# One packet for the categories, row groups loaded first, and the weight loads shared out differently

## What is computed

```python
def _L0_cond_ref(x, cat_ids, W, b):
    selected_W = W[cat_ids]
    selected_b = b[cat_ids]
    return jnp.einsum('bsd,bdh->bsh', x, selected_W) + selected_b[:, None, :]

x = x + _L0_cond_ref(x, itok_B_0_63, L0_cond_W, L0_cond_b)
```

## Time and profile before

| | |
|---|---|
| median of 3 runs | 105.71 us (105.23 to 106.25) |
| the profiled execution, device time | 105.33 us |
| its span in the profile | 103.6 us |
| TensorE busy | 87.4 us |
| DMA | 31.26 MB, 302 GB/s over the span |
| granted TensorE clock | full in every slice |

### The profile page before, as it was taken

How to read it: one execution, slowest core, us unless ns; L and a number is a source line. 1 busy time by engine, 2 the same in 40 slices (tenths; PEclk the granted TensorE clock), 3 DMA queues, 4 the chain that set the end, 5 groups by cost and what they waited for, 6 DMA issues and landing times.

```text
span 103.6 us, 3047 instructions
## 1 busy us (share of the span) xinstructions
PE 87.4 (84%) x786; PEld 58.2 (56%) x786; DVE 57.0 (55%) x137; ACT 55.0 (53%) x97; POOL 62.0 (60%) x103
## 2 busy tenths in 40 slices
PE   0039958867889977979999999999999999999990
PEld 0017725534555745637576767666667676666650
DVE  1085514233998879075646463737292828282841
ACT  0001927326436609279577665766666757585600
POOL 5000019889989898999999998984053597000000
PEclk9999999999999999999999999999999999999999
DMA  0587994999999999999999999999997799993353
GB/s 10 143 273 220 291 314 167 334 324 331 354 332 350 353 347 345 348 356 399 351 391 372 394 367 400 373 388 350 373 392 271 227 333 320 331 322 114 108 202 105
DMA packets 13825, 31.26 MB, mean 302 GB/s; under 512 B 1840, under 2 KB 7664, under 8 KB 13808
## 3 DMA queue, kind: packets, MB, share of 16 engines
q0 software_dynamic: 7456, 25.17, 69.0%
q1 hardware_dynamic: 4832, 4.59, 13.5%
q10 hardware_dynamic: 1520, 1.31, 4.4%
HBM read 25.30 MB, written 8.39 MB: 325 GB/s over the span
## 4 chain that ended last, share of the span: by engine, by line
PE 54%; DMA 16%; issue 15%; POOL 6%; POOLq 3%; DVE 2%; ACT 1%; ACTq 0%; SPq 0%; DVEq 0%
PE mm_ps L527 36%; DMA w_all<-in_L_cond_W 12%; PE xt_ps L444 10%; PE mm_ps L513 6%; POOL w_all L162 5%; DMA cat_col_i<-in_itok_B 4%; POOLq L162 2%; PE xt_ps L527 2%; POOL rows L171 1%; POOLq L156 1%; ACT w_slot L292 1%; DVE rows L413 0%; DVE same_ahead L361 0%; DVE has_place L373 0%; PE mm_ps L458 0%
## 5 line engine op out<-in xcount | busy, mean ns | idle before, releaser
L527 PE MATMUL mm_ps<-w_slot,xT 128*64 128x256 f32 x496 | 57.8, 380 | 5.3 <-ACT w_slot L292 4.0
L292 ACT COPY w_slot<-w_all 128x512 f32 x64 | 38.7, 620 | 32.8 <-SPq L207 20.7
L527 PEld LDWEIGHTS mm_ps<-w_slot,xT 128*64 128x64 f32 x496 | 34.5, 137 | 22.9 <-issue 4.9
L162 POOL DMA_DIRECT2D w_all<-in_L_cond_W x56 | 33.4, 599 | 9.8 <-SPq L207 5.6
L413 DVE TENSOR_TENSOR rows<-mm_ps,rows 128x512 f32<-128x512 f32 (+1 forms) x32 | 21.6, 674 | 23.9 <-PE mm_ps L527 23.0
L292 DVE COPY w_slot<-w_all 128x512 f32 x64 | 26.6, 447 | 12.1 <-SPq L207 12.1
L444 PE MATMUL xt_ps<-ident,rows 128*128 128x128 f32 x128 | 19.0, 298 | 0.4 <-DMA rows<-in_x 0.4
L171 POOL DMA_DIRECT2D rows<-in_x x14 | 11.0, 786 | 13.5 <-SPq L207 12.9
L444 PEld LDWEIGHTS xt_ps<-ident,rows 128*128 128x128 f32 x128 | 15.3, 151 | 6.5 <-issue 5.3
L304 ACT COPY xT<-xt_ps 128x512 f32<-128x512 f32 x32 | 17.1, 584 | 0.0
L175 POOL DMA_DIRECT2D out<-rows x22 | 16.1, 736 | 1.1 <-issue 1.1
(11 more groups left out here) (39 smaller groups left out, 13.3 us busy)
## 6 DMA issues: line engine op xcount, KB each, us to landing
w_all<-in_L_cond_W POOLq DMA_DIRECT2D x56, 256.0 KB
rows<-in_x POOLq DMA_DIRECT2D x14, 512.0 KB, 8.1
out<-rows POOLq DMA_DIRECT2D x22, 256.0 KB, 7.0
out<-rows SPq DMA_DIRECT2D x8, 256.0 KB, 3.7
rows<-in_x SPq DMA_DIRECT2D x2, 512.0 KB, 4.5
w_all<-in_L_cond_W ACTq DMA_DIRECT2D x4, 256.0 KB, 4.8
w_all<-in_L_cond_W SPq DMA_DIRECT2D x4, 256.0 KB, 5.8
out<-rows SPq DMA_DIRECT2D x2, 128.0 KB, 1.7
```

Source lines behind the costliest of these rows:

```text
L162: engine.dma_start(w_all[:, n, :, :], weights[bass.ds(c, 1), :, :].rearrange("c (k p) h -> p (c k) h", p=P), **how).then_inc(first_w_loade ...
L292: copy(w_slot[:, PAIR * p + half, :, :].rearrange("p k h -> p (k h)"), w_all[:, bass.ds(c, 1), :, :].rearrange("p c k h -> p (c k h)")).th ...
L527: last = T.matmul(to[HALF * half:HALF * (half + 1), :], xT[:, slot, k, j, :], w_slot[:, j, k, :], start=False, stop=(k == K - 1), skip_gro ...
```

## The change

The categories come once, as one row of 128 numbers on one partition (`cats_i`, SyncE). VectorE casts them to bf16, and two small matmuls spread them in PSUM: `cat_row` (128x128, by a row of ones) and `cat_col_ps` (128x1). VectorE and the later plan steps read these from PSUM. The row of ones is made by VectorE and copied by ScalarE at the very start. `cat_col_i` and its transfer are gone.

SyncE issues the rows of groups 0, 1 and 2 with the bias, without a wait between them. Loads 0 and 2 are ScalarE's, 1 and 3 SyncE's; GpSimd has all loads from 4 on, and begins when one load is reported. GpSimd reads the next packed word one load ahead. It stores a whole group by one transfer of 524,288 bytes. Rows of groups 5 and 6 come after loads 25 and 31 (24 and 29 before), and the stores of groups 0 to 4 come later in the order of loads. From load 12 on a load waits for the one eight before it. Groups 11 to 15 are stored as before.

```diff
-FIRST_X = 2
-FIRST_LOADS = 8
-REPORTED_FIRST = 5
+FIRST_X = 3
+FIRST_LOADS = 4
+REPORTED_FIRST = 1
-X_AFTER_LOAD = {3: 13, 4: 19, 5: 24, 6: 29, 7: 33, ...}
-STORE_AFTER_LOAD = {0: 33, 1: 37, 2: 40, 3: 43, 4: 46, 5: 51, 6: 59}
+X_AFTER_LOAD = {3: 13, 4: 19, 5: 25, 6: 31, 7: 33, ...}
+STORE_AFTER_LOAD = {0: 37, 1: 40, 2: 43, 3: 46, 4: 48, 5: 51, 6: 59}
...
-            sp.dma_start(cat_row_i[:, :], cat.partition_broadcast(P)).then_inc(cats_loaded, 16)
+            sp.dma_start(cats_i[:, :], cat.rearrange("(a b) -> a b", a=1)).then_inc(cats_loaded, 16)
             load_rows(sp, 0)
             sp.dma_start(bias_nat[:, :], bias).then_inc(bias_loaded, 16)
-
-            sp.wait_ge(cats_loaded, 32)
             for g in range(1, FIRST_X):
                 load_rows(sp, g)
...
-            def store_group(g):
-                for q in range(QUADS_IN_GROUP * g, QUADS_IN_GROUP * (g + 1)):
-                    pool.wait_ge(sums_added, q + 1)
-                    store_quad(pool, q, stored[g % X_SLOTS])
+            def store_sums(g):
+                pool.wait_ge(sums_added, QUADS_IN_GROUP * (g + 1))
+                store_group(pool, g)
...
             pool.wait_ge(w_loads_done, REPORTED_FIRST)
-            load_rows(pool, FIRST_X)
             for n in range(FIRST_LOADS, C):
                 if n % WORD == 0 and n > FIRST_LOADS:
-                    word = words_read(...)
+                    word = next_word
+                if n % WORD == WORD - 1 and n + 1 < C:
+                    next_word = list_word(n // WORD + 1)
...
-            act.dma_start(cat_col_i[:, :], cat.rearrange("(b a) -> b a", a=1)).then_inc(cats_loaded, 16)
-
-            act.wait_ge(cats_loaded, 32)
-            load_weights(act, 0, words_read(mybir.EngineType.Activation, cat_row_i[0:1, 0:1], C - 1)[0])
+            act.wait_ge(ones_set, 1)
+            nc.scalar.copy(ones_row[:, :], ones_f[:, :]).then_inc(ones_ready, 1)
+
+            act.wait_ge(cats_loaded, 16)
+            load_weights(act, 0, words_read(mybir.EngineType.Activation, cats_i[0:1, 0:1], C - 1)[0])
...
-            dve.wait_ge(cats_loaded, 32)
-            step(V.tensor_copy(cat_col[:, :], cat_col_i[:, :]))
+            dve.wait_ge(cats_loaded, 16)
+            V.tensor_copy(cats[:, :], cats_i[:, :]).then_inc(plan_step, 1)
+            dve.wait_ge(plan_products, 1)
+            step(V.tensor_copy(cat_col[:, :], cat_col_ps))
...
+            pe.wait_ge(plan_step, PLAN_STEPS["cats"])
+            pe.wait_ge(ones_ready, 1)
+            T.matmul(cat_row, ones_row[:, :], cats[:, :], start=True, stop=True)
+            T.matmul(cat_col_ps, cats[:, :], ones[0:1, :], start=True, stop=True).then_inc(plan_products, 1)
```

More of the change, by code:

```diff
@@ L29 @@
 FAR = 1000.0
-PLAN_STEPS = {"samples": 6, "first": 9, "list": 12, "slots": 15, "bias": 16}
-X_AFTER_LOAD = {3: 13, 4: 19, 5: 24, 6: 29, 7: 33, 8: 37, 9: 40, 10: 43, 11: 46, 12: 48, 13: 51, 14: 55, 15: 60}
-STORE_AFTER_LOAD = {0: 33, 1: 37, 2: 40, 3: 43, 4: 46, 5: 51, 6: 59}
+PLAN_STEPS = {"samples": 6, "cats": 7, "first": 10, "list": 13, "slots": 16, "bias": 17}
+X_AFTER_LOAD = {3: 13, 4: 19, 5: 25, 6: 31, 7: 33, 8: 37, 9: 40, 10: 43, 11: 46, 12: 48, 13: 51, 14: 55, 15: 60}
+STORE_AFTER_LOAD = {0: 37, 1: 40, 2: 43, 3: 46, 4: 48, 5: 51, 6: 59}
 POOL_GROUPS = 11
@@ L67, in build_cond_residual @@
     out_pairs = out.rearrange("(t h) s d -> (h s) t d", h=PAIR)
+    out_groups = out.rearrange("(g p h) s d -> g (h s) p d", p=PAIRS_IN_GROUP, h=PAIR)
     with ExitStack() as ctx:
@@ L89, in build_cond_residual @@
         ones = sb("ones", [P, 1], BF16)
+        ones_f = sb("ones_f", [1, P])
         powers = sb("powers", [P, WORD])
-        cat_row_i = sb("cat_row_i", [P, B], I32)
-        cat_col_i = sb("cat_col_i", [P, 1], I32)
+        cats_i = sb("cats_i", [1, B], I32)
+        cats = sb("cats", [1, B], BF16)
+        ones_row = sb("ones_row", [1, P], BF16)
         cat_col = sb("cat_col", [P, 1])
@@ L124, in build_cond_residual @@
         loads_ps = mm_ps[1][0:1, 0, LIST_WORDS:LIST_WORDS + 1]
+        cat_row = mm_ps[3][:, 0, 0:B]
+        cat_col_ps = mm_ps[3][:, 0, B:B + 1]
         bias_ps = [mm_ps[r % BANKS][0:ROWS, 0, :] for r in (2, 4, 6, 8)]
@@ L131, in build_cond_residual @@
         consts_ready = sem("consts_ready")
+        ones_set = sem("ones_set")
+        ones_ready = sem("ones_ready")
         plan_step = sem("plan_step")
@@ L166, in stores_until @@
         def stores_until(g):
-            return 16 * QUADS_IN_GROUP * (g // X_SLOTS + 1)
+            return 16 * (g // X_SLOTS + 1)
         def load_rows(engine, g):
@@ L176, in store_quad, with store_group @@
                              rows[:, g % X_SLOTS, PAIR * n:PAIR * (n + 1), :]).then_inc(done, 16)
+        def store_group(engine, g):
+            engine.dma_start(out_groups[g], rows[:, g % X_SLOTS, :, :]).then_inc(stored[g % X_SLOTS], 16)
         def store_pair(engine, p, done):
@@ L240, in _, with list_word @@
                       allow_small_or_imprecise_dtypes=True).then_inc(consts_ready, 1)
[L241 to L245 removed]
+            def store_sums(g):
+                pool.wait_ge(sums_added, QUADS_IN_GROUP * (g + 1))
+                store_group(pool, g)
+            def list_word(w):
+                return words_read(mybir.EngineType.Pool, load_words[0:1, w:w + 1], 2 ** (WORD * BITS) - 1)[0]
             pool.wait_ge(plan_read, 1)
[L249 to L250 removed]
+            word = list_word(FIRST_LOADS // WORD)
             pool.wait_ge(w_loads_done, REPORTED_FIRST)
[L253 removed]
             for n in range(FIRST_LOADS, C):
                 if n % WORD == 0 and n > FIRST_LOADS:
[L256 to L257 removed]
+                    word = next_word
+                if n % WORD == WORD - 1 and n + 1 < C:
+                    next_word = list_word(n // WORD + 1)
                 if n == CERTAIN_LOADS:
@@ L275, in _ @@
                     if after == n:
-                        store_group(g)
+                        store_sums(g)
             for g in range(len(STORE_AFTER_LOAD), POOL_GROUPS):
-                store_group(g)
+                store_sums(g)
         def slots_of(engine, g, half):
@@ L347, in _ @@
             V = nc.vector
+            V.memset(ones_f[:, :], 1.0).then_inc(ones_set, 1)
             V.memset(ones[:, :], 1.0).then_inc(plan_step, 1)
@@ L356, in _ @@
             assert steps[0] == PLAN_STEPS["samples"]
-            dve.wait_ge(cats_loaded, 32)
-            step(V.tensor_copy(cat_col[:, :], cat_col_i[:, :]))
+            dve.wait_ge(cats_loaded, 16)
+            V.tensor_copy(cats[:, :], cats_i[:, :]).then_inc(plan_step, 1)
+            steps[0] += 1
+            assert steps[0] == PLAN_STEPS["cats"]
+            dve.wait_ge(plan_products, 1)
+            step(V.tensor_copy(cat_col[:, :], cat_col_ps))
             dve.wait_ge(consts_ready, 2)
-            step(V.scalar_tensor_tensor(out=same_ahead[:, :], in0=cat_row_i[:, :], scalar=cat_col[:, 0:1],
+            step(V.scalar_tensor_tensor(out=same_ahead[:, :], in0=cat_row, scalar=cat_col[:, 0:1],
                                         in1=is_ahead[:, :], op0=ALU.is_equal, op1=ALU.mult,
@@ L375, in _ @@
             step(V.tensor_scalar(place[:, :], place_ps, FAR, first_here[:, 0:1], ALU.add, ALU.mult))
-            dve.wait_ge(plan_products, 2)
+            dve.wait_ge(plan_products, 3)
             V.tensor_copy(load_words[:, :], mm_ps[1][0:1, 0, 0:LIST_WORDS + 1]).then_inc(plan_read, 1)
-            V.tensor_scalar(same[:, :], cat_row_i[:, :], cat_col[:, 0:1], None, ALU.is_equal).then_inc(plan_step, 1)
+            V.tensor_scalar(same[:, :], cat_row, cat_col[:, 0:1], None, ALU.is_equal).then_inc(plan_step, 1)
             V.tensor_scalar(place_powers[:, :], powers[:, :], place[:, 0:1], None, ALU.mult).then_inc(plan_step, 1)
```

10 lines of the change are left out of this document (5 added, 5 removed).

## The result

The changed kernel took 102.33 us (median of 4 runs, 101.54 to 103.11) against 105.66 us; its ratio to the kernel before is 0.9656, 95% interval 0.9575 to 0.9736. The profiled execution took 101.54 us, the shortest of the four, and 99.9 of them are its span.

The account below looks back on a forecast made before the run. Load 31's landing, set by the bytes ahead of it, plus 0.91 us and a 58.09 us tail bounds the span. Landing 4.7 us earlier gives 98.9 us, with 1.73 outside it 100.6 us; range 99.0 to 103.2.

Parts of the forecast that it names:

- part 4: Load 31's landing: at 39.9 us against 44.60, a gain of 4.7 us, with bounds of 3.6 and 5.8.
- early transfers stay poor: Rival, 17 in 100: early DMA stays slow and most of the early gain is lost; time about 103 us.
- The bound: Whole kernel: the span is load 31's landing, plus 0.91 us to its matmul, plus 58.09 us of tail.
- Part 1, the order of bytes: Weight queue: group 6 rows behind load 31 and no category broadcast leave 11.60 MB ahead of load 31, 0.59 MB gained.
- Part 2, the early filling: First 19 us: data from 3.2 us at 300 GB/s, 342 from 12 us on; 5.03 MB moved against 3.99.
- part 3: GpSimd's start: plan ready at 5.7 us, GpSimd starts at about 8.6, its first data come at 10.5; the hole is closed.
- the cover I had reckoned: Early queue: SyncE's and ScalarE's 2.69 MB last until 12.2 us, covering GpSimd's first data at 10.5 by 1.7 us.
- the price of the packet: Category steps of the plan: they cost nothing under the cover; without it each microsecond would cost one.
- Part 5, TensorE's own row: Groups 0 to 4: without waits TensorE is ready at 38.9 us, loads allow 40.8, so loads decide by 1.9.
- Part 6, nothing late next: After load 31: load 37 has 2.7 us of slack, group 10 rows come at 57.9 us, wanted at 62; store and word zero.
- The signs: Right: no hole at 15-17 us, GpSimd's load at 8-9, over 4.7 MB by 19 us. Wrong: under 300 GB/s after 12.
- Slower by the low clock: Rival, 5 in 100: TensorE stays at its lower level, 4.0 us more for each such group; three give about 108 us.

Follow-up runs that it names:

- experiment 1: The changed kernel with the kernel before's tables: rows of groups 5 and 6 behind loads 24 and 29, stores where they were; 103.86 us, ratio 0.9844.
- experiment 2: The kernel before with only the change's two tables for the order of rows and stores; 104.28 us against 105.42, ratio 0.9906.
- experiment 8: The changed kernel with rows of group 2 issued by GpSimd behind load 7, and no wait of GpSimd for a reported load before load 4; 100.18 us.
- experiment 5: The changed kernel with rows of group 2 issued by GpSimd behind load 7, not by SyncE ahead of the weights; 101.46 us, ratio 0.9669.
- Experiments 8 and 11: The changed kernel with rows of group 2 behind load 7 and no gate for GpSimd, measured on two chips; 100.18 us, then 99.83 us.
- Experiment 7: The changed kernel with the old category transfers (broadcast and column) and ScalarE's table load behind its loads again; 104.90 us against 105.34, ratio 0.9966.
- experiment 9: The kernel before with only the change's categories (one packet, spread by TensorE) and rows of group 1 not waiting for them; 104.24 us against 105.87.
- experiment 6: The changed kernel with two stores for a group, as before, and no word read ahead; 101.95 us, ratio 0.9692.
- experiment 3: The changed kernel without GpSimd's wait for a reported load before load 4; median 101.78 us over seven runs, in two heaps.

## Why the prediction was right, and where it was off

The forecast was 100.6 us, 5.1 below the median of before; measured are 102.33, 3.3 below it. The mechanism held, and the size was too large: 102.33 lies outside the 99.5 to 101.7 that the bounds of part 4 gave, and inside the range only by the room left for the rival "early transfers stay poor". Part of this is spread: the profiled execution (101.54) is the shortest of the four, 0.8 below their median, and it misses the forecast by 0.9. The repeat on another chip gave 101.60, a gain of 4.3. The sum is checked against the profiled execution below.

**The bound** (load 31, 0.91 us, a tail of 58.09 us) held to the last tenth: 0.91 and 58.1 us in the changed kernel, and 58.9 to 59.0 for the two together in every experiment whose load 31 the chain shows.

**Part 1, the order of bytes:** 1.5 us by the sum; experiment 1 shows 1.5 us by the medians and 1.7 to 2.7 by the gains, experiment 2 shows 1.1. Right.

**Part 2, the early filling,** is the term that was mis-sized. I took 300 GB/s from 3.2 to 12 us and 342 after that, 5.03 MB by 19 us; 4.81 MB were moved. The first half was even better than assumed (311 GB/s from 4 to 11 us), but from 12 to 19 us, where I had taken 342, there were 285, and 292 in the repeat. The 0.22 MB are 0.65 us. The rate after that was 338 to 339 and not 342 (0.2 us), and together with the remainder of the table load 31 landed at 40.89 and not at 39.9.

The sentence behind the 342 is in part 3: GpSimd "issues 262 KB in 0.71 us (2.82 / 4), 372 GB/s, faster than 342". That is the pace inside one burst. It leaves out GpSimd's pauses between bursts; with them ten loads took 8.64 us, 303 GB/s, in the change and in its repeat. From about 12 us on, when the bytes queued by SyncE and ScalarE were used up, the DMA engines then had no more than that to move. In experiment 8 GpSimd's pace was 346 GB/s, and 342 were moved from 12 to 19 us. In experiment 5 the pace was the same 346, but only 316 were moved. No experiment changed the pace alone, so this cause is argued and not shown.

**Part 3, GpSimd in time:** the plan came earlier than thought (4.94 us, not 5.7), since the packet landed 1.4 us after its issue, below the lower end of my bounds, 1.7. But the gate did not open with SyncE's last issue. I had priced load 0 at nothing; it took 5.80 us (5.37 to 5.80 in four executions), because it shares the DMA engines with three row groups (4.84 us with two, experiment 5). So GpSimd started at 9.90 and not at 8.6 us. That is inside the cover I had reckoned (10.3 us), but the queue emptied sooner than I thought: 2.69 MB were queued, and at the rates of the windows they were moved by about 11.3 us, not 12.2, since the early rate was above 300. GpSimd's first data, 1.9 us behind 9.90, came at 11.8. Experiments 8 and 11, where GpSimd starts at 6.6 us, moved 0.4 to 0.5 MB more by 19 us.

**Part 3, the price of the packet.** "The new steps of the plan cost nothing" is right in the changed kernel. That the early categories are worth something I had put in the row of the first data only (0.8 us between 3.2 and 4.0). Experiment 7 shows that without them 2.6 to 2.9 us are lost, since load 0, the gate and SyncE's loads all hang on them. But alone, in the kernel before, they give some 1.6 us (experiment 9). So neither the categories nor the rest makes the gain alone; each needs the other. The prediction gave the packet no such price.

**Part 5, TensorE's own row:** the last pair of group 0 was to start at 16.9 us and started at 17.74. From there 3 x 5.64 + 5.04 gives 39.7, and with a 1.00 us wait for VectorE 40.7, against 41.80 by the load. The loads still decide, by 1.1 us and not by 1.9.

**Part 6, nothing late next:** right; the chain shows no wait behind 41.80 us. One store in place of two and the word read ahead: no difference in experiment 6.

**The signs.** The hole from 15 to 17 us was gone, 4.81 MB were moved by 19 us, load 31 landed at 40.89 us and the tail was 58.1. But GpSimd's first load did not come at 8 to 9 us, and one sign of being wrong did appear: under 300 GB/s after 12 us (285 until 19 us). It belongs to the term that was too large.

**The rivals.** "Poor early transfers" was the nearest, and the measured gain lies between it and the forecast. "Slower by the low clock" did not come in the changed kernel (a mean granted clock of 0.983 at the lowest in its four runs), but TensorE's lower level did appear in experiment 3: it cost 2.2 us in the profiled execution (24 matmuls in 5.06 us, in place of 2.81). The Trainium skill, "TensorE: Matmul & The Clock Gate" (section "HAM oscillation — how this bites in real kernels"), describes it as transfer waits that make TensorE cold again; experiment 3 agrees, with a granted clock of 0.54 behind a stretch in which TensorE was busy for 1.34 of 4.70 us. On the rule that the prediction drew from the Trainium skill, "DMA: Bandwidth & Descriptors" (section "SWDGE vs HWDGE vs iDMA"), against giving loads 4 to 7 to GpSimd: four loads were issued in 2.88 us from 12.64 us on, beside copies of VectorE at 13.33 and 15.13 us. That is 0.72 us each, as for the single load at 23.61 us with no such copy beside it, and no loss by a lock is seen.

## What to carry to other kernels

Where a kernel is first bound by transfers and then by one engine without gaps, look for the one transfer at which the bound changes: its landing sets the end, and it is a matter of the bytes ahead of it and of the holes in the early queue. Take the pace of the engine that issues the transfers from a long stretch with its pauses, not from one burst. Move bytes that are not needed yet behind it, and price every gate in the first microseconds by the landing of the transfer that opens it, beside all that shares the DMA engines with it. A transfer that others wait for should not share with what is wanted later. Taking away the gate alone gave two heaps, about 99.8 and about 102.3 us; with the third row group out of the way as well all eight runs stayed between 99.54 and 100.66 us.

## What the runs showed of the hardware

- A packet of 512 bytes, the first transfer of the kernel, landed 1.4 us after its issue (0.88 to 2.30, the changed kernel). The same numbers spread over 128 partitions took 3.6 and 4.1 us, and the column 5.04 us with three row groups behind it.
- Load 0 took 4.84 us behind two row groups (experiment 5) and 5.37 to 5.80 behind three. Of the first four loads the slowest took 5.8 us in the change, 9.05 us when GpSimd issued beside them behind three row groups (experiment 3), and 4.7 and 6.7 us when it did so behind two (experiments 8 and 11). Since the reports are counted in order, one late load held back all behind it.
- TensorE's granted clock fell to half (0.54 in the window) after a stretch with little work (busy for 1.34 of 4.70 us, experiment 3), and the 24 matmuls behind it took 5.06 us in place of 2.81. The first transposes go at 0.22 to 0.25 us each in every kernel, against 0.128 later, with a granted clock shown as full; that was not explained.
- GpSimd issued a weight load of 262 KB in about 0.72 us and a row group of 524 KB in 0.77 to 0.95 us (the change and its repeat): its price goes by the transfer more than by the byte.
